# Alternating additive attention rows with the next batch's head rows in pairs, with split norms and a diagonal per row

## What is computed

```python
# L0: gated sum over neighbours; score * sum(h), leaky; done for all 8 batches at once, before the rest
# L1: 4 heads of dot-product attention, joined by Wo, then one more attention, then an affine norm
scores = einsum('nd,md->nm', h, h); scores = where(adj or eye, scores, -1e16)
out = softmax(scores) @ h + b
# L2, L3: additive attention
e = left[:, None] + right[None, :]; e = leaky(e)          # slope 0.01 (L2), 0.2 (L3)
out = softmax(where(mask, e, -inf)) @ h                   # L2: adj or eye; L3: adj alone
```

## Time and profile before

| | |
|---|---|
| runs | 6500.03, 6510.92, 6516.5 us, median 6510.92 |
| profiled execution | 6511.56 us, its span 6509.8 us, mean granted clock 0.942 |
| busy | PE 88%, DVE 68%, ACT 60%, POOL 25% of the span |
| L0 and the mask | to 361.9 us |
| heads of the first batch | to 810 us |
| one batch of the loop | 758 to 761 us, seven times |
| the rest (epilogue) | from 6107 us |

### The profile page before, as it was taken

The page is one execution under the profiler, slowest core; times in us unless marked ns, Lnnn a source line. Parts: engine busy times, 40 slices in busy tenths (PEclk is TensorE's granted clock), DMA queues, the critical chain, the costliest instruction groups (busy, mean ns, idle before and its releaser), DMA issues.

```text
span 6509.8 us, 163090 instructions
## 1 busy us (share of the span) xinstructions
PE 5744.7 (88%) x52064; PEld 4654.5 (71%) x52064; DVE 4424.1 (68%) x7928; ACT 3901.8 (60%) x5701; POOL 1599.2 (25%) x1239
## 2 busy tenths in 40 slices
PE   7689898998989888998989989898889989899866
PEld 4268676886768777786768867687777867688655
DVE  4756476766766676766767667766767677676765
ACT  1056457666666656666576666666566675766655
POOL 0100014023230413104140231304131041402354
PEclk9889899999999999999989999999999999899988
DMA  4200000000000000000000000000000000000000
GB/s 137 64 5 2 1 5 2 2 2 9 5 2 2 2 11 2 2 2 4 10 2 2 2 9 5 2 2 3 11 2 2 2 4 9 2 2 2 8 1 4
DMA packets 99234, 55.58 MB, mean 9 GB/s; under 512 B 89424, under 2 KB 92752, under 8 KB 98384
## 3 DMA queue, kind: packets, MB, share of 16 engines
q1 hardware_dynamic: 60496, 34.71, 1.9%
q10 hardware_dynamic: 37888, 9.97, 0.7%
HBM read 35.75 MB, written 8.91 MB: 7 GB/s over the span
## 4 chain that ended last, share of the span: by engine, by line
PE 67%; issue 9%; DVE 9%; ACT 5%; DVEq 3%; POOL 1%; ACTq 0%; DMA 0%; SPq 0%; POOLq 0%
PE tp L878 23%; PE po L898 23%; PE pss L869 7%; PE pss L868 7%; DVE rows L1172 3%; DVEq L237 3%; ACT pss L1039 2%; DVE pt L1184 2%; ACT rows L1060 2%; PE px L829 2%; PE px L825 1%; PE tp L887 1%; PE px L843 1%; PE px L835 1%; DVE tmp L254 1%
## 5 line engine op out<-in xcount | busy, mean ns | idle before, releaser
L878 PE MATMUL tp<-ident,rows 128*128 128x128 f32 x14336 | 2054.5, 285 | 181.6 <-DVE pt L1184 89.7
L1184 DVE COPY pt<-tp 128x512 f32<-128x512 f32 x2048 | 1336.5, 686 | 1287.7 <-PE tp L878 1272.5
L878 PEld LDWEIGHTS tp<-ident,rows 128*128 128x128 f32 x14336 | 1609.7, 144 | 592.0 <-issue 554.9
L1060 ACT ACTIVATE rows<-rows,nm 128x2048 f32<-128x2048 f32 x896 | 1797.5, 2006 | 265.4 <-DVE nm L1172 257.5
L898 PE MATMUL po<-pt,hn 128*64 128x128 f32 x28672 | 1887.0, 288 | 0.5 <-DVE pt L1184 0.2
L898 PEld LDWEIGHTS po<-pt,hn 128*64 128x64 f32 x28672 | 1667.8, 145 | 164.7 <-issue 164.7
L707 POOL TENSOR_TENSOR rows<-sr,mask 128x2048 f32<-128x2048 f32 x256 | 1046.4, 4088 | 697.3 <-PE tp L878 679.2
L1012 ACT COPY pt<-tp 128x512 f32<-128x512 f32 x1536 | 850.7, 589 | 449.1 <-PE tp L878 429.2
L868 PE MATMUL pss<-ha 128*128 128x512 f32 x2560 | 1067.8, 417 | 24.6 <-issue 15.3
L869 PE MATMUL pss<-ha,hb 128*128 128x512 f32 x2560 | 1015.3, 397 | 0.0
L1172 DVE CUSTOM_DVE_ANT_0 rows<-pss,mask,nm 128x1024 f32<-128x1024 f32 x640 | 821.7, 1284 | 202.6 <-issue 201.4
(11 more groups left out here) (102 smaller groups left out, 3375.0 us busy)
## 6 DMA issues: line engine op xcount, KB each, us to landing
adjb<-in_adj SPq DMA_DIRECT2D x32, 512.0 KB, 4.6
xin<-x SPq DMA_DIRECT2D x9, 512.0 KB, 4.2
xb<-in_x ACTq DMA_DIRECT2D x16, 256.0 KB, 3.4
x<-t ACTq DMA_DIRECT2D x16, 256.0 KB, 2.7
xb<-x SPq DMA_DIRECT2D x8, 512.0 KB, 4.2
out<-xb SPq DMA_DIRECT2D x32, 128.0 KB, 2.0
xtp<-in_xt SPq DMA_DIRECT2D x12, 256.0 KB, 6.6
ab<-in_a ACTq DMA_DIRECT2D x16, 64.0 KB, 3.3
```

The costliest lines, as they stand in the source:

```text
L878: last = nc.tensor.transpose(tp[row.bank[q]][:, r * P:(r + 1) * P], rows[:, row.slot, jb * P:(jb + 1) * P], ident[:])
L1060: nc.scalar.activation(rows[:, row.slot, :], rows[:, row.slot, :], ACT.Exp, scale=-1.0, bias=nm[:, row.t, 1:2], accum_out=rs[:, row.t:row. ...
L1184: nc.vector.tensor_copy(pt[:, CH * q:CH * (q + 1), row.k % SLOTS, :], tp[row.bank[q]][:].rearrange("p (j n) -> p j n", n=P)).then_inc(pt_d ...
```

## The change

- The order of rows in `LOOP` is written out by `loop_order`, in pairs of rows: 8 pairs of GAT2, 7 pairs of the heads, then 8 times (one pair of ADD1, one pair of the heads), 5 pairs of the heads, 4 times (one pair of ADD2, three pairs of the heads), and the 4 pairs of ADD2 that are left. `AHEAD` is 8: the first eight GAT2 rows of the next batch belong to the end of the body, and no "after" tasks are left. All task steps are set anew.
- The GAT2 norm has four pieces, `la` (leaky, mean, centre), `lb` (variance), `lc` (centre of x + y), `ld` (variance); `norm_start` becomes `center` and `variance`. The products with `rstd` and `gam`, the sums with `bet` and x move from VectorE to GpSimd.
- `open` and `close` are gone. Each ADD2 row gets `diag` added to its 128 columns on GpSimd, behind `mask_row`.
- GpSimd does `finish` ahead of the tasks. Row statistics (`nm`, `rs`, `rc`) go by the position in the segment, `place`.
- The epilogue has 7 empty steps between units instead of 5, and a tail of 8 steps.

```diff
-AHEAD = 4
+AHEAD = 8
+TAIL = 8
 GAP = 5
+END_GAP = 7
...
+def loop_order():
+
+    heads = [pair for u, hn in ((0, 1), (1, 2), (2, 1), (3, 2)) for pair in pairs_of(u, hn)]
+    first, second = pairs_of(ADD1, 0), pairs_of(ADD2, 0)
+    order = pairs_of(GAT2, 2) + heads[0:7]
+    for n in range(8):
+        order += [first[n], heads[7 + n]]
+    order += heads[15:20]
+    for n in range(4):
+        order += [second[n]] + heads[20 + 3 * n:23 + 3 * n]
+    return order + second[4:]
...
+    for c in range(NC):
+        n, m = CH * c, (0, 1, 3, 4)[c]
+        tasks += [(8 + m, "xn", 0, c), (9 + m, "proj", 0, c), (10 + m, "hn", 0, c)]
+        tasks += [(8 + n, "la", GAT2, c), (9 + n, "lb", GAT2, c), (11 + n, "lc", GAT2, c), (12 + n, "ld", GAT2, c)]
+        tasks += [(14 + n, "xt", ADD1, c), (14 + n, "h", ADD1, c), (15 + n, "r", ADD1, c)]
+        tasks += [(22 + 3 * c, "proj", 1, c), (23 + 3 * c, "hn", 1, c)]
+        tasks += [(44 + 4 * c, "proj", 2, c), (45 + 4 * c, "hn", 2, c)]
+        tasks += [(71 + 3 * c, "proj", 3, c), (72 + 3 * c, "hn", 3, c)]
+        for unit in (ADD1, ADD2):
+            end = at(order, unit, n + CH - 1)
+            tasks += [(end + 5, "ra", unit, c), (end + 6, "rb", unit, c)]
+        tasks += [(63 + 2 * c, "xt", ADD2, c), (63 + 2 * c, "h", ADD2, c), (64 + 2 * c, "r", ADD2, c)]
+    end = [at(order, H - 1, CH * c + CH - 1) for c in range(NC)]
+    last = end[NC - 1]
+    tasks += [(end[0] + 6, "z0", GAT2, 0), (end[0] + 7, "z1", GAT2, 0)]
+    tasks += [(end[1] + 6, "z0", GAT2, 1), (end[1] + 7, "z1", GAT2, 1)]
+    tasks += [(last + 1, "proj", GAT2, 0), (last + 2, "z0", GAT2, 2), (last + 3, "z1", GAT2, 2)]
+    tasks += [(last + 4, "hn", GAT2, 0), (last + 4, "proj", GAT2, 1), (last + 5, "hn", GAT2, 1)]
+    tasks += [(last + 5, "proj", GAT2, 2), (last + 6, "hn", GAT2, 2)]
+    tasks += [(last + 6, "z0", GAT2, 3), (last + 7, "z1", GAT2, 3), (last + 7, "proj", GAT2, 3), (last + 8, "hn", GAT2, 3)]
+    return Segment(order, True, True, tasks)
...
+                if name == "lb":
+                    nc.gpsimd.tensor_tensor(yc, yc, spread(rstd, CH), ALU.mult)
+                    drain_link(pool)
+                    nc.gpsimd.tensor_tensor(yc, yc, each(gam), ALU.mult)
+                    drain_link(pool)
+                    nc.gpsimd.tensor_tensor(yc, yc, each(bet), ALU.add)
+                    if c == 0:
+                        xb_c.n += 16
+                        wait(xb_c)
+                    drain_link(pool)
+                    nc.gpsimd.tensor_tensor(xbc, xbc, yc, ALU.add).then_inc(mid_ready, 1)
+                elif name in ("ld", "rb"):
+                    nc.gpsimd.tensor_tensor(xbc, xbc, spread(rstd, CH), ALU.mult)\
+                      .then_inc(x_done if unit == ADD2 else x_ready, 1)
...
+                nc.gpsimd.tensor_tensor(rows[:, row.slot, :], sr[:], mask[:, row.t, :], ALU.add)
+                drain_link(pool)
+                own = rows[:, row.slot, row.t * P:(row.t + 1) * P]
+                nc.gpsimd.tensor_tensor(own, own, diag[:, row.t, :], ALU.add).then_inc(mr_ready, 1)
```

More of the change, by code:

```diff
@@ L61, in __init__ @@
         self.gat = unit <= GAT2
-        self.odd, self.pair = k % 2 == 1, k // 2
+        self.odd, self.pair, self.place = k % 2 == 1, k // 2, k % NB
         self.bank, self.before = {}, {}
 class Segment:
-    def __init__(self, units, gap, carried, ahead, tasks):
+    def __init__(self, order, carried, ahead, tasks):
         self.first = AHEAD if carried else 0
-        self.rows, self.tasks, self.starts = [], {}, []
-        self.blocks = len(units) * NB
+        self.rows, self.tasks = [], {}
+        self.blocks = sum(2 for pair in order if pair)
         k = n_gat = n_add = act_tiles = dve_tiles = 0
         if ahead:
-            units = units + [(GAT2, 2)]
-        for n, (unit, hn) in enumerate(units):
-            if n and (gap == "all" or (gap == "last" and n == len(units) - 1)):
-                self.rows += [None] * GAP
-            self.starts.append(len(self.rows))
-            for t in range(NB if k < self.blocks else AHEAD):
+            order = order + pairs_of(GAT2, 2)[:AHEAD // 2]
+        for pair in order:
+            if not pair:
+                self.rows.append(None)
+                continue
+            unit, hn, first = pair
+            for t in (first, first + 1):
                 row = Row(unit, t, hn, k)
@@ L115, in __init__ @@
         self.dve_tiles = sum(r.copier.count("dve") for r in own)
-        self.steps = range(self.first, len(self.rows) + (0 if ahead else AHEAD + 1))
+        self.steps = range(self.first, len(self.rows) + (0 if ahead else TAIL))
         for step, name, unit, c in tasks:
             self.tasks.setdefault(step, []).append((name, unit, c))
-        assert all(k in ("before", "after") or k in self.steps for k in self.tasks), self.tasks.keys()
+        assert all(k == "before" or k in self.steps for k in self.tasks), self.tasks.keys()
         turns = [(self.rows[AHEAD - 2], q) for q in (2, 3)] if carried else []
@@ L726, in run_segment @@
             def run_segment(segment):
-                for task in segment.tasks.get("before", ()):
-                    run_task(segment, *task)
                 for s in segment.steps:
@@ L928, in run_segment @@
                         turn(turned, 3)
-                for task in segment.tasks.get("after", ()):
-                    run_task(*task)
                 exp_c.n += segment.blocks
@@ L1206, in run_segment @@
                     if row:
-                        if row.unit == GAT2 and row.t == 0 and segment is LOOP:
-                            wait(diag_c, diag_c.n + TASKS("close") + 1)
-                        if row.unit == GAT2 and row.t == CH:
-                            wait(diag_c, diag_c.n)
                         masked_scores(row, 0)
```

166 lines of the change are left out of this document (59 added, 107 removed).

## The result

The kernel after takes 6775.9 us (median of four runs, 6768.2 to 6782.9) where the kernel before takes 6509.9: 1.0397 times as long, with an interval of 1.0376 to 1.0417. That is 266 us slower, outside the predicted range (6310 to 6570) and on the other side of no change. The profiled execution took 6772.2 us, its span is 6770.3.

What follows compares the result with a forecast made beforehand. TensorE bounds head rows, a ScalarE chain additive rows. Terms -11 - 5 - 3 + 2 + 4 = -13 us a batch, rounded to 12.5; 7 x 12.5 = 87 us off about 6511 gives 6425 us, range 6370 to 6490.

Steps and rivals of the forecast that it cites:

- What bounds the kernel: Head rows bound by TensorE, additive rows by a ScalarE chain; TensorE waits 2.5 us for `ot` in nearly each additive pair.
- Interleaving: Additive and head rows alternating in pairs, 12 groups a batch: 24.8 us a group, gain 11 us a batch, bounds 4 and 23.
- the clock: In the mixed groups, a rival: lone gaps pass at full clock, group 23.8 us, total 6336 us; chance 0.22.
- rival C: Mixed groups: half clock also catches the next head row's dot products; slower, +8 us a batch, 6567 us; chance 0.21.
- Eight rows carried over: At the loop's end, moving ADD2's last norm inside the body gains 5 us per jump, seven jumps.
- the jump: The loop body's jump back: its row interval should fall from 14.2 to 9 us, the jump's own 3.6 us staying.
- Norms in pieces: GAT2 and h0: norm work split and partly moved from VectorE to GpSimd, gain 3 us a batch, bounds 0 and 8.
- Diagonal: ADD2 rows: the added GpSimd operation per row stays covered, zero effect, bounds -1 and 14 us.
- Tasks moved: h1's projection moved into head rows, +2 us a batch; GAT2's next-batch tasks squeezed into eight ADD2 rows, +4 us.
- the tail: Steps 104 to 111, eight ADD2 rows holding GAT2's next-batch tasks: +4 us a batch, bounds 0 and 11.
- rival B: Steps 104 to 111: squeezed tasks use up the other gains, net 0, 6510 us; chance 0.15.
- The epilogue: After the loop: the same work, with 7 instead of 5 empty steps following the same dependency; priced at zero.

Runs made afterwards that it cites:

- the kernel in pairs with projections last: The kernel after with one edit, the projection put last among the tasks of its step: 6624.0 us, ratio 1.0177.
- the better runs: The kernel after with additive units in runs of 16, projections last, and the additive norms' sum and centring one step later: 6667.6 us, ratio 1.0235.
- the smaller kernel: The kernel before with norm products on GpSimd, ADD1's last eight rows paired with h1's first eight, h1's projection ending four steps earlier: 6431.2 us, ratio 0.987.

## Why the prediction was wrong, point by point

**What bounds the kernel: right.** The wait for `ot` is there 117 times as before, 310 us in all where near 290 was forecast.

**Interleaving: the mechanism was right, the size is inside the bounds, and the clock is luck.** The eight groups of the alternating stretch of ADD1 in the kernel after, one window each:

```profile
3409.74:3436.60 26.86, 22.32 (x213) 18.29 (x210) 18.29 (x31) 18.46 (x26) 10.32 (x7) 0.94 0.00 1
3436.60:3460.44 23.84, 19.88 (x214) 16.93 (x210) 16.67 (x29) 16.45 (x23) 9.48 (x6) 1.00 0.01 2
3460.44:3484.34 23.90, 19.94 (x214) 16.90 (x210) 19.34 (x35) 16.53 (x23) 9.87 (x8) 1.00 0.01 2
3484.34:3509.67 25.33, 21.35 (x220) 17.44 (x216) 18.18 (x31) 18.27 (x27) 10.90 (x6) 1.00 0.01 2
3509.67:3543.10 33.43, 26.81 (x223) 21.71 (x220) 23.90 (x37) 18.55 (x28) 10.96 (x8) 0.85 0.01 1
3543.10:3570.10 27.00, 22.59 (x215) 18.67 (x213) 18.18 (x31) 18.28 (x27) 9.54 (x6) 0.94 0.01 2
3570.10:3597.24 27.14, 23.11 (x220) 18.91 (x216) 20.59 (x37) 18.35 (x27) 9.81 (x8) 0.94 0.01 2
3597.24:3621.19 23.95, 21.12 (x216) 18.11 (x214) 16.74 (x29) 13.58 (x21) 2.81 (x4) 1.00 0.01 2
```

At full clock and without tasks a group takes 23.8 to 24.0 us, the 23.8 of the prediction's working. The fourth and the sixth have the same instructions on VectorE and ScalarE and differ in the clock, 1.00 against 0.94: 25.33 and 27.00 us, 1.67 apart, 0.4 of it a longer gap of TensorE (2.93 against 2.54 us). The eighth takes 23.95 us here and 25.6 at 0.93 in the batch before. I had reckoned 1.6 from the value matmuls. But the half clock can cost more. The third group of the batch before, the same instructions and the same two gaps of TensorE (2.46 and 1.21 us) as the 23.90 us above:

```profile
2664.49:2691.09 26.60, 22.80 (x214) 19.32 (x210) 19.34 (x35) 16.52 (x23) 9.88 (x8) 0.87 0.01 2
```

That is 2.7 us more and past the 25.9 us from which on my rival C turns the sign. Which group is caught isn't foretold by its own gaps. In the batch shown four of eight pass at full clock, in all seven 22 of 56, and in the kernel in pairs with projections last only 8 of 56; there the fifth group falls to 27.3 us, and the stretch is no shorter for it (212.7 us against 211.45), since the first three run at 0.87 to 0.93. Read as I had read it, the rule of the Trainium skill ("TensorE: Matmul & The Clock Gate", "HAM oscillation": every burst after an idle gap begins cold) does not hold for the groups at full clock; the page tells it of a kernel that waits longer between its bursts. The fifth group, 33.43 us, has the held-up centring. In the end the twelve groups give 6 us a batch against the better runs, where 11 was forecast, between my bounds of 4 and 23, with the reserve on that 6 said above. Two things stay open: why the four groups of the smaller kernel gave nothing, and how much of the 44 us is the clock.

**Eight rows carried over: right for the jump, wrong for its consequence.** In the batch shown the jump's interval is 9.9 us (3216.66 to 3226.54), 14.2 before, 9 forecast. But the carry is also what doubled the tasks of GAT2's steps 9 to 13, and with these mended it is worth 1 us a batch at most, not 5. I had read the new steps as numbers of a list and not asked what had moved them.

**Norms in pieces: mis-sized.** Taken as -3 us a batch with a bound of 8; alone in the kernel before it is -13. I had taken what was left of GAT2's and h0's time after other causes as the most that VectorE's lateness could cost. The trace of that kernel shows 5.5 us less in GAT2, 4.6 in h0, and 1.7 in ADD1 and 1.2 in h1, where I had looked for nothing; ADD2 is as it was.

**Diagonal: the price was near enough in this kernel (2 us a batch, zero forecast, inside -1 to 14), the reason incomplete.** I asked whether GpSimd would be last in its step; it was not. I didn't ask what its shifted operations would then lie beside. (The add itself lasts 0.57 us with the way to it, where I had 0.89.)

**Tasks moved: the step that failed.** I gave +6 us a batch, with 11 as the upper bound of the tail. Measured: a batch is 29 us longer; with 13 gained by the norms, 6 by the alternation and 4 at the jump, the tasks cost some 52. That is a balance, not a measurement: it takes the effects as if they added up, and holds the 6 us a batch of the fifth group's held-up centring as well. Measured by runs of their own are the twelve tasks of h0 in the kernel before (16 a batch), the order within a step (22) and transpose and projection of ADD1 apart (9 to 10). The tail's 11 and the head rows' 6 to 8 are read from windows. I priced a task by TensorE's own time ("16 chunk tasks of roughly 1 us") and noticed two tasks of `px` in a step only in steps 104 to 111. The price of a task is how long the bank stays taken. From the start of a projection to the end of VectorE's second subtraction that is 4.4 us at step 9 (3230.65 to 3235.09) and 6.4 at step 12, and in TensorE's list all that stands behind the next task of the bank waits with it. The numbers for it were at hand: the casts in the earlier trace rows, and the position of VectorE's tasks behind its scores.

**The tail.** Steps 104 to 111 of the batch shown, the forecast's mark for rival B being 9 us: 7.9, 6.3, 12.6, 9.9, 8.8, 9.2, 8.6 and 5.4. One of these steps, TensorE and ScalarE of the kernel after:

```profile
3913.57 0.45 PE L922 MATMUL tp<-ident,ot 128*128 128x128 f32 x1 [2.44 <-ACT ot L1053]
3913.95 0.69 PE L870 MATMUL px<-ident,whf 64*128 64x64 f32 x4
3915.43 3.75 PE L860 MATMUL px<-xz,wo 128*128 128x512 f32 x4 [0.79 <-ACT hn L1020]
...
3919.31 0.58 ACT L1015 CAST ha<-px 64x512 fp32r<-64x512 f32 x1 [4.18 <-PE px L860]
```

The projection of GAT2 has four matmuls that take 3.75 us behind the gap before the turn back, and ScalarE can't begin its three casts before they end: the tasks lie on TensorE's and ScalarE's path one after the other. By the mark of 9 us three of the eight steps show B, a fourth and a fifth come near it, and the eight together cost 11 us a batch, its full bound. It was only a fifth of what the tasks cost. No run moved these tasks (the eight rows take 68.6 us in every kernel that has them so), so that their price is read and not tested.

**The epilogue: failed too.** "The same work", priced at zero, cost 31 us more, and 36 came back with the old gaps and the old steps of its tasks.

**Rival C.** It had the right sign and 6567 us, 209 us short. Its mechanism is there: a group without tasks takes 26.6 us where the clock falls to 0.87. It isn't what made the kernel slower: in runs it is slower still, by 44 us once the centrings are free.

## What to carry to other kernels

A small task that shares a buffer costs the time until the buffer is free again, over every engine that reads it, and not the time of its own instruction. When a list of tasks is moved, write down for each step which of them share a buffer and who releases it, and put the one with the longest release last. Before comparing two orders, look for instructions that last several times longer than their kind: here they made one order look 131 us worse where about 44 were its own. The best version found changes least: the norms' products on an idle engine, at the old steps, 1.4% faster than before.

## What the runs showed of the hardware

A 256-wide VectorE instruction with two inputs in SBUF (0.43 us) did not end before a 4.1-us GpSimd addition of the mask that had begun ahead of it. The addition of the first pair of lines above ends at 3458.83, the centring at 3459.11, 0.28 us behind it. Over the eighteen traces there are 673 such instructions; 659 ended 0.28 or 0.29 us behind the addition, however early they began, and the other 14 began in its last tenth of a microsecond. It is a wait for the whole operation, not a slowdown. VectorE's copies from PSUM and its masked scores, which read PSUM and SBUF, kept their 0.69 and 1.2 to 1.3 us beside the same additions. This is the rule that the prediction had weighed from the Trainium skill ("SBUF — State Buffer", section "Who interferes with whom"), there with GpSimd operations of 0.70 us, by which it could cost 5 us a batch; these runs agree with the rule, and the partner that mattered was the 4.1-us addition that was there before the change, whose place against VectorE's instructions the change moved.

TensorE lost clock in GAT2 and h0 of the kernel after (0.93 and 0.94) where gaps of 3.5 to 5.4 us stood, and kept 1.00 in h0 when they went: of the 10.6 us that the order in a step gave back in GAT2 (125.88 to 115.26), TensorE's busy time accounts for 3.6 (109.71 to 106.14), the rest is waiting.
